# Layer 0's tile pipeline: experts two steps behind the top-k search, and a new order on each engine

## The reference, cut to what matters

```python
x = x + attn(norm(x))            # its output projection @ Wo + bo is in the changed stage
x = x + xattn(norm(x), ctx)      # Q = h @ Wq.T + bq, 16 heads of 16; K, V from ctx (77 rows)
#   scores = Q @ K.T / 4;  the 32 largest of 77 are kept: top_k(scores, 32)
#   softmax over those 32, weights @ V, then @ Wo.T + bo
x = x + ffn(norm(x))             # logits = h @ router_w.T + router_b; 8 experts
#   y = h @ expert_w[argmax].T + expert_b[argmax], times max(softmax(logits))
```

## Time and profile before

| | us |
|---|---|
| median of 3 runs | 1982.43 (1979.96 to 1985.38) |
| the profiled execution | 1987.05 |
| its span, first to last instruction | 1985.3 |

### The profile page before, as it was taken

How to read it: one execution, slowest core, us unless ns; L and a number is a source line. 1 busy time by engine, 2 the same in 40 slices (tenths; PEclk the granted TensorE clock), 3 DMA queues, 4 the chain that set the end, 5 groups by cost and what they waited for, 6 DMA issues and landing times. The chain is left out here.

```text
span 1985.3 us, 27618 instructions
## 1 busy us (share of the span) xinstructions
PE 1579.4 (80%) x8891; PEld 871.2 (44%) x8892; DVE 1255.1 (63%) x4695; ACT 934.1 (47%) x1831; POOL 482.1 (24%) x386
## 2 busy tenths in 40 slices
PE   4758999999976488889867676999987882389993
PEld 2431222222224366767656432333326761156662
DVE  6988888887407999999980356777735558401112
ACT  2731777777655445555543340666673651111110
POOL 3760000000003354455542151111111342300003
PEclk9965999999897778888878785999998995689997
DMA  6175133331010000000000059336300121741003
GB/s 196 59 203 79 21 45 44 44 45 20 25 43 1 1 1 2 1 1 1 1 1 1 6 163 170 43 44 86 44 1 1 15 41 32 254 162 33 26 24 93
DMA packets 113013, 102.91 MB, mean 52 GB/s; under 512 B 45095, under 2 KB 88171, under 8 KB 112878
## 3 DMA queue, kind: packets, MB, share of 16 engines
q1 hardware_dynamic: 111345, 97.06, 22.6%
q0 software_dynamic: 1536, 4.20, 0.7%
HBM read 67.61 MB, written 33.35 MB: 51 GB/s over the span
## 5 line engine op out<-in xcount | busy, mean ns | idle before, releaser
L1052 DVE TENSOR_REDUCE arena<-banks 128x2 f32<-128x1024 f32 (+1 forms) x448 | 481.2, 1108 | 149.7 <-PE banks L899 94.3
L988 ACT ACTIVATE arena<-banks 128x512 f32<-128x512 f32 (+3 forms) x896 | 439.9, 557 | 187.3 <-PE banks L938 180.6
L899 PE MATMUL banks<-arena 96*128 96x512 bf16 (+3 forms) x896 | 285.9, 396 | 50.1 <-DVE arena L1052 21.2
L938 PE MATMUL banks<-arena 98*128 98x512 bf16 (+3 forms) x896 | 272.0, 364 | 9.0 <-ACT arena L988 6.8
L950 PE MATMUL banks<-arena 128*32 128x512 f32 (+3 forms) x1792 | 220.8, 565 | 12.6 <-ACT arena L988 6.5
L1654 DVE MATCH_REPLACE8 arena<-arena 128x77 f32<-128x77 f32 x1024 | 213.9, 226 | 0.0
L899 PEld LDWEIGHTS banks<-arena 96*128 96x128 bf16 x896 | 80.6, 102 | 233.7 <-DVE arena L1052 136.9
L938 PEld LDWEIGHTS banks<-arena 98*128 98x128 bf16 x896 | 82.4, 98 | 188.0 <-ACT arena L988 124.1
L2433 DVE COPY arena<-banks 128x1024 f32<-128x1024 f32 x23 | 28.2, 1225 | 206.9 <-PE banks L2372 206.9
L1549 POOL TENSOR_SCALAR arena<-arena 128x256 f32<-128x256 f32 x32 | 39.1, 1223 | 476.2 <-DVE arena L1635 476.1
L1650 DVE MAX8 arena<-arena 128x8 f32<-128x77 f32 x1024 | 149.5, 225 | 1.4
(11 more groups left out here) (276 smaller groups left out, 2535.2 us busy)
## 6 DMA issues: line engine op xcount, KB each, us to landing
arena<-parts SPq DMA_DIRECT2D x192, 128.0 KB, 7.3
arena<-in_L_ffn_W SPq DMA_DIRECT2D x16, 1024.0 KB, 12.2
parts<-arena SPq DMA_DIRECT2D x24, 512.0 KB, 9.1
v<-arena SPq DMA_DIRECT2D x32, 256.0 KB, 2.3
arena<-v SPq DMA_DIRECT2D x16, 512.0 KB, 11.1
arena<-sorted SPq DMA_DIRECT2D x23, 128.0 KB, 2.1
expert_out<-arena SPq DMA_DIRECT2D x23, 128.0 KB, 1.7
sorted<-arena SPq DMA_DIRECT2D x5, 512.0 KB, 7.4
```

Source lines behind the costliest of these rows:

```text
L899: mm = pe.matmul(bank[:, 0:w], qst[r][0:KS, j, i * P:(i + 1) * P], kst[r][0:KS, j, kb * BANK:kb * BANK + w], start=True, stop=not diag)
L938: pe.matmul(bank, kst[r][0:KM, j, kt * P:(kt + 1) * P], qst[r][0:KM, j, half * BANK + lo:(half + 1) * BANK], start=True, stop=True).then_i ...
L988: act.activation(prob[:, gi % 2 * G + j, lo:BANK], PS[:, 4 + n % 3, 0:BANK - lo], ACT.Exp, scale=SCALE).then_inc(sem(s + "_exp"), 1)
L1052: dve.tensor_reduce(m2[u % 2][:, 2 * pair:2 * pair + 2, i, kb], PS[:, 2 * (n % 2):2 * (n % 2) + 2, 0:w], AX.X, ALU.max).then_inc(sem(s + " ...
```

## The change

- Experts move from four to two steps behind the search, the rest of the cross attention to one step. FIRST is -2, LAST is T + 3: 21 passes. x1 is made two tiles ahead of the search instead of three; `normal` makes h1 and h2 a step after their statistics; x2's statistics are taken in the step of its `output`.
- The order of every engine in a step is new. TensorE now does h2 and `logits`, projection, weights, `context`, h1, `turn_context`, `query`, choice and spread, `scores`, spread, mixed, `output`, and `experts` last.
- On VectorE `largest` is split in `largest` (the maxima) and `taken` (the striking out), and the small work is placed between them.
- The experts write to bank 1 (EB), and the logits to bank 7; waits follow.
- The expert matrices are turned 3, 3 and 2 in three steps.
- Last in a step ScalarE takes an exponential of one column into `warm`, so that the table of the exponential is loaded there.
- `choose` subtracts with a tensor operation in place of one with a scalar operand.

The core of the diff, with TensorE's and ScalarE's new order:

```diff
+            warm = R.f32(1)
...
-            PB, WB, QB, OB = 3, 4, 6, 7
-            FIRST, LAST = -3, T + 4
+            EB, PB, WB, QB, OB = 1, 3, 4, 6, 7
+            FIRST, LAST = -2, T + 3
+            TURNS = (3, 3, 2)
...
-                return [w for w, n in ((0, t + 2), (1, t - 3)) if inside(n)]
+                return [w for w, n in ((0, t + 2), (1, t - 1)) if inside(n)]
...
+            def turned(t):
+
+                n = t - FIRST
+                return range(sum(TURNS[:n]), sum(TURNS[:n + 1]))
...
+                    if inside(t - 2):
+                        turn_h2(t - 2)
+                        logits(t - 2)
+                    if inside(t + 2):
+                        turn_attended(t + 2)
+                        project(t + 2)
+                    for e in turned(t):
+                        turn_expert(e)
+                    if inside(t - 1):
+                        for c in range(4):
+                            turn_weights(t - 1, c)
+                        context(t - 1)
+                    if inside(t + 1):
+                        turn_h1(t + 1)
+                    if inside(t - 1):
+                        turn_context(t - 1)
...
+                        turn_choice(t - 2)
+                        turn_spread(t - 2, 0)
+                        turn_spread(t - 2, 1)
...
+                        turn_spread(t - 2, 2)
+                        turn_spread(t - 2, 3)
+                    if inside(t - 1):
+                        turn_mixed(t - 1)
+                        output(t - 1)
...
+                        experts(t - 2, 0)
+                        experts(t - 2, 1)
...
+                    if inside(t - 2):
+                        turned_h2(t - 2)
+                    if inside(t + 2):
+                        attended(t + 2)
+                        attended_rows(t + 2)
+                    for e in turned(t):
+                        act.wait_ge(sem(s + "_wep"), e + 1)
+                        act.copy(WeT[:, e].rearrange("p k n -> p (k n)"), PS[:, WB + e % 2, :]).then_inc(sem(s + "_weT"), 1)
+                    if inside(t - 1):
+                        for c in range(4):
+                            copy_weights(t - 1, c)
+                        context(t - 1)
+                    if inside(t + 1):
+                        turned_h1(t + 1)
+                        queries(t + 1)
+                    if inside(t - 2):
+                        router_exp(t - 2)
+                        choice(t - 2)
+                        copy_spread(t - 2, 0)
+                        copy_spread(t - 2, 1)
+                    if inside(t + 1):
+                        copy_scores(t + 1)
+                    if inside(t - 2):
+                        copy_spread(t - 2, 2)
+                        copy_spread(t - 2, 3)
+                    if inside(t):
+                        exp_all(t)
+                    if inside(t - 1):
+                        mixed(t - 1)
+                        mixed_rows(t - 1)
...
+                        gated(t - 2)
...
+                        act.activation(warm, eps1, ACT.Exp).then_inc(sem(s + "_warm"), 1)
+                        act.wait_ge(sem(s + "_warm"), t + 1)
...
+                    if normed(t - 1):
+                        pool.wait_ge(sem(s + "_rstd"), steps(t - 1))
+                    if inside(t - 2):
+                        if t >= 4:
+                            pool.wait_ge(sem(s + "_hp2"), t - 3)
+                        normal(h2[t % 2], t - 1, 1).then_inc(sem(s + "_h2"), 1)
+                    if inside(t + 1):
+                        if t >= 1:
+                            pool.wait_ge(sem(s + "_hp1"), t)
+                        normal(h1[(t + 1) % 2], t - 1, 0).then_inc(sem(s + "_h1"), 1)
...
+                        largest(t, 0)
+                        taken(t, 0)
+                    if inside(t - 2):
+                        router(t - 2)
+                        choose(t - 2)
+                        chosen(t - 2)
+                    if inside(t):
+                        largest(t, 1)
+                        taken(t, 1)
+                    if inside(t):
+                        largest(t, 2)
+                    if inside(t - 1):
+                        sums(t - 1)
+                        normalize(t - 1)
+                    if inside(t):
+                        taken(t, 2)
+                    if inside(t - 2):
+                        gates(t - 2)
+                    if inside(t):
+                        largest(t, 3)
                     if normed(t):
                         row_statistics(t)
-                    if inside(t - 4):
-                        choose(t - 4)
-                    if normed(t):
                         aggregate(t)
-                    if inside(t - 4):
-                        chosen(t - 4)
                     if inside(t):
-                        largest(t, 0)
-                    if inside(t - 2):
-                        sums(t - 2)
+                        taken(t, 3)
```

More of the change, by code:

```diff
@@ L1313, in logits @@
                     for k in range(KD):
-                        mm = pe.matmul(PS[:, QB, D:D + E], h2T[t % 2][:, k, :], wr[0][:, k, :], start=(k == 0), stop=(k == KD - 1))
+                        mm = pe.matmul(PS[:, OB, 0:E], h2T[t % 2][:, k, :], wr[0][:, k, :], start=(k == 0), stop=(k == KD - 1))
                     mm.then_inc(sem(s + "_lp"), 1)
@@ L1471, in gated @@
                         act.wait_ge(sem("e0_x"), t - 1)
-                    act.activation(yt[t % 2], PS[:, OB, 0:D], ACT.Identity, scale=gate[t % 2]).then_inc(sem(s + "_yt"), 1)
+                    act.activation(yt[t % 2], PS[:, EB, 0:D], ACT.Identity, scale=gate[t % 2]).then_inc(sem(s + "_yt"), 1)
                 def exp_all(t):
@@ L1505, in _ @@
+                    if inside(t - 1):
+                        mixed(t - 1)
+                        mixed_rows(t - 1)
                     if normed(t):
                         deviations(t)
-                    if inside(t + 1):
-                        copy_scores(t + 1)
-                    if inside(t + 3):
-                        attended_rows(t + 3)
-                    for e in range(2 * (t - FIRST), 2 * (t - FIRST) + 2):
-                        if e < E:
-                            act.wait_ge(sem(s + "_wep"), e + 1)
-                            act.copy(WeT[:, e].rearrange("p k n -> p (k n)"), PS[:, WB + e % 2, :]).then_inc(sem(s + "_weT"), 1)
@@ L1529, in _ @@
-                    if inside(t - 4):
-                        gated(t - 4)
-                    if inside(t - 1):
-                        copy_weights(t - 1, 2)
-                        copy_weights(t - 1, 3)
-                    if inside(t):
-                        exp_all(t)
-                    if inside(t + 2):
-                        turned_h1(t + 2)
-                    if inside(t - 3):
-                        turned_h2(t - 3)
-                    if inside(t - 1):
-                        context(t - 1)
+                    if inside(t - 2):
+                        gated(t - 2)
@@ L1650, in largest, with taken @@
                         dve.max(m8[r][:, k, hd, :], src[:, hd, :]).then_inc(sem(s + "_m" if k == 0 else f"{s}_m{k}"), 1)
+                def taken(t, k):
+                    r, hn = t % 2, t * NH
+                    src = (sc if k == 0 else left)[r]
                     dve.wait_ge(sem(s + "_m" if k == 0 else f"{s}_m{k}"), hn + NH)
```

155 lines of the change are left out of this document (40 added, 115 removed).

## The result

| | before | after |
|---|---|---|
| median of the timed runs | 1983.91 (4 runs) | 2050.07 (4 runs, 2049.08 to 2052.46) |
| the profiled execution | 1987.05 | 2049.95 |

The ratio is 1.0329, with a 95% interval of 1.031 to 1.0347. The forecast was 2054 us, range 2005 to 2088.

The account below looks back on a forecast made before the run. VectorE bound the kernel before; afterwards a TensorE loop through ScalarE would, at 34.2 us a pass. Search ending 102 us later, less 31 from a shorter tail, gave +71 on 1982.4: about 2054 us, range 2005 to 2088.

Parts of the forecast that it names:

- The closed loop on TensorE: TensorE's work plus its waits for ScalarE's fixed order bound a pass: 29.7 us at full clock, 34.2 with slow clock.
- the small ones: TensorE's waits at `project`, `turn_weights` with `context`, `turn_context` and `turn_choice` behind ScalarE copies: 3.4 us a pass together.
- TensorE's work at full clock: TensorE's matmul work in one pass, if at 2.4 GHz throughout: about 20.1 us.
- The clock: Two idle stretches of about 3 us a pass bring TensorE to half clock: 4.5 us a pass taken, of 7.
- The loop without it: TensorE's pass of work and waits at 2.4 GHz throughout: 29.7 us, total about 1982; as a rival, 8%.
- The passes: Search passes of 23.6, 25.6 and 31 us, twelve of 34.2, a last of 31; search ends 102 us later.
- VectorE: Searches about 26.3 us a pass, idle some 5 us at x2's statistics and 2 ahead of the router.
- Start: TensorE has three turns, not two, ahead of the second tile's projection: first top-k 3 us later, at about 611.
- The tail: Stage's end after the last top-k, one pass and tile 15's experts: 54 us against 85, 31 back.
- The table load: ScalarE's exponential table load behind `gated`: 1.28 us on the loop, nothing saved, no drain; drain rival 2072 us, 3%.
- The small edits: Subtraction written as a tensor operation and banks exchanged: taken as nothing, bounded by 0.17 us a step either way.
- VectorE stays the bound: Rival: ScalarE and TensorE finish sooner, a pass is VectorE's 26.3 us: 39 us faster, 1944 us; 9%.

Follow-up runs that it names:

- run 1: Changed kernel with ScalarE's `gated` copy one pass later, behind h2's copy: 1991.07 us, 1.0032 of the kernel before.
- run 2: Changed kernel with ScalarE's exp_all moved behind `mixed`, ahead of mixed_rows: 2004.43 us, 1.011 of the kernel before.
- run 5: Changed kernel with `gated` one pass later and exp_all behind `mixed`: 1964.88 us, 0.9903 of the kernel before.
- run 6: Changed kernel with `gated` one pass later, exp_all behind `mixed`, and VectorE's x1 and x2 statistics behind the last `taken`: 1944.23 us, 0.9804 of before.
- run 4: Changed kernel with idle transposes on TensorE, 20 ahead of `logits` and 18 ahead of `output`: 2000.58 us, 1.0094 of the kernel before.
- run 3: Changed kernel with only VectorE's statistics of x1 and x2 moved behind the tile's last `taken`: 2048.6 us, 1.033 of the kernel before.

## Why the prediction was right, step by step

- *The closed loop on TensorE.* Right, and shown by runs 1, 2, 5 and 6: two instructions of a half idle engine, moved in its order, give back 85 us. The pass was put at 34.2 and is 34.1, but luck has a part in that, since two terms missed and cancelled. The waits were added up to 9.6 us a pass and are 8.2. `logits` 3.15 for 3.4 and `output` 2.61 for 2.8 are close; the small ones were put at 3.4 and are 2.4. TensorE's work at full clock was put at 20.1 and is 21.7 in run 6, at a clock of 1.00 (in run 4, without its transposes, 21.2). I had taken 3.5 us off the step of before for its 7.1 at half clock; 23.1 of work there at 0.87 against these 21.7 and 21.2 makes it 1.4 to 1.9.
- *The clock.* I took 4.5 us a pass between bounds of 0 and 7; run 4 gives 4.3, and TensorE's work in after, 25.9, is 4.2 above that of run 6. The 4.5 was a choice between the bounds, not worked out. The loop without it was put at 29.7 and is 29.9 with the stretches filled, by the same two misses. That both stretches cost, neither at full price, was right; 0.85 is below the 0.87 of before, as said.
- *The passes.* 23.7, 25.8, 31.6, then eleven of 33.8 to 34.8 and one of 31.2, against 23.6, 25.6, 31 and twelve of 34.2. The last tile's search took 28.5, not 31: TensorE has no query or scores of a later tile in that pass, and VectorE doesn't wait for x2. With the start, the search ended 92 us later than before where 102 were forecast; less 1.6 us more outside the stage and 0.2 in the tail, that is the 8 us between 62.9 and the forecast's 71.
- *VectorE.* Idle at the statistics and at the router about as forecast (4.5 and 2.7 a pass against 5 and 2). The pass of 26.3 that it would have as the bound, 25.4 + 0.9, is what run 6 measures.
- *Start.* Mis-sized: 3 us were forecast. From the landing of the expert weights to the first search it is 15.65 us (590.75 to 606.4) against 15.1 (592.98 to 608.08), 0.6 more, and they landed 2.2 us sooner. That need not be the change's doing: in the twelve experiments, with the same start, it lies between 588.6 and 592.6 us, and the first search began between 604.2 and 610.5.
- *The tail.* 54.2 us from the last search's end to the end of the last `gated` (1122.4 to 1176.6), 54 forecast, 85 before.
- *The table load.* 896.17 + 1.28 is 897.45, and the warm exponential begins at 897.46: no drain, as the earlier trace rows had it. The Trainium skill (ScalarE: Activation LUTs, What ACT_TABLE_LOAD costs) adds about 1.38 us to every switch; no row here shows it, behind the load or ahead of it (`gated` ends at 896.16, the load begins at 896.17).
- *The small edits.* Mis-sized, though nothing came of it here: bounded at 0.17 us a step, while the subtraction in `choose` took 0.95 more than that. The step that failed is that I bounded it by the length of a like instruction in a quiet place; the trace of before had five of the 16 in a GpSimd operation already, up to 1.85 us long. In after VectorE waits anyway; in run 5 the pass is 1 us longer than in run 6, where it isn't held.
- *The rivals.* "VectorE stays the bound" would have been 1944 us. It is what the kernel becomes once the two instructions and the statistics are moved: run 6, 1944.23, with a pass of 26.3. The Trainium skill (Perfetto Trace Analysis, Identifying the Most-Contended Engine) would have the busiest engine looked at first. In after that is VectorE still, 265.7 us of 341.4. Its busy share doesn't say that it waits for a loop in which it has no part, and run 3, which eased its order, gave nothing. Of the changed kernels the traces agree with the rule for runs 5 and 6, once the loop is gone.

## What to carry to other kernels

Before an order by hand is taken, follow the engine that has its longest work last in a pass round to its first wait of the next: where each of those waits leads back to that engine itself, the sum of its work and its waits is a bound of the pass, however idle the engine waited for is. On that second engine, put nothing that the first needs soon behind an instruction that waits for the longest work. `gated` one pass later and exp_all one place later turned 3.3% slower into 1.0% faster (run 5), and with the statistics moved too it was 2.0% (run 6). Idle stretches of TensorE of about 3 us on such a loop cost more than themselves, through the clock, so a microsecond of idling taken away gave 1.6 to 3 (4.1 for 2.5 in run 1, 3.4 for 1.1 in run 2).

## What the runs showed of the hardware that was not expected

- A small VectorE instruction in one of two forms (TENSOR_TENSOR with both operands from the arena, TENSOR_SCALAR on the arena) that begins under a GpSimd tensor operation of two operands is held until that one ends: on 128x8 1.43 and 1.44 us in place of 0.17 and 0.22. The router's sum of the arena with a bank (0.15) and a reduction (0.16) are not held by the same GpSimd operation. The scalar form is held even where it reads one operand from the arena and its two scalars are constants. In an earlier stage of after 11 of 16 are held, at 0.98 us for 0.19. All 16 of the line, and then one of them with GpSimd's operation beside it, which ends at 57.91, 0.04 ahead of VectorE's:

```profile
L676 DVE TENSOR_SCALAR arena<-arena x16: 190/982/992, 44.5 to 105.8; 128x48 f32<-128x48 f32 x16
```

```profile
56.97 0.98 DVE L676 TENSOR_SCALAR arena<-arena 128x48 f32<-128x48 f32 x1
```

```profile
56.81 1.10 POOL L512 TENSOR_TENSOR arena<-arena 128x512 f32<-128x512 f32 x1
```

  So for the scalar form the number of operands in the arena is not the condition. The Trainium skill (SBUF — State Buffer, Who interferes with whom) says that a VectorE instruction with two SBUF inputs contends with a GpSimd instruction that reads SBUF, and calls the port pair that they share an exclusive lock. The rows agree for the tensor form. For the scalar form it names the modes that take both ports as the case; the rows show the hold and not the mode.
- With no idle stretch of TensorE above 1.50 us in a pass its mean clock is 1.00 (run 6) or 0.98 (run 5), with two of about 3 us 0.85 (after), with one of 2.61 0.90 (run 1), with one of 2.8 beside one of 1.5 0.92 (run 2).
